# A linear attention stage rewritten: rotary sum in place in PSUM, state updates a unit ahead, head sums in four quarters, an own order for each engine

## What is computed

```python
q, k, v = x @ Wq.T, x @ Wk.T, x @ Wv.T            # 16, 4 and 4 heads of 128
q = q * cos + rotate_half(q) * sin                # k likewise
qf, kf = elu(q) + 1, elu(k) + 1
# scan over the tokens, causal, per head:
state = state + kf[:, None] * v[None, :]
z = z + kf
out = (qf @ state) / (qf @ z + EPS)
x = layernorm(x + out @ Wo.T)
x = layernorm(x + ffn(x))      # Hadamard, up and gate, silu, Hadamard, down
```

## Time and profile before

| | us |
|---|---|
| median of 3 runs (2710.3 to 2711.7) | 2710.74 |
| the profiled execution | 2705.35 |
| its span, first to last instruction | 2703.6 |

### The profile page before, as it was taken

The page is one execution under the profiler, slowest core; times in us unless marked ns, Lnnn a source line. Parts: engine busy times, 40 slices in busy tenths (PEclk is TensorE's granted clock), DMA queues, the critical chain, the costliest instruction groups (busy, mean ns, idle before and its releaser), DMA issues. The chain is left out here.

```text
span 2703.6 us, 32657 instructions
## 1 busy us (share of the span) xinstructions
PE 2523.3 (93%) x10689; PEld 1933.0 (71%) x10689; DVE 1671.2 (62%) x2283; ACT 1042.8 (39%) x1820; POOL 782.5 (29%) x661
## 2 busy tenths in 40 slices
PE   4899999999999999959999968999999999999997
PEld 3566666666666666638888857888888888888886
DVE  7587878787878787866767744443434343444444
ACT  2455555555555555532333323322222222222221
POOL 4365656565656565631112100000000000000000
PEclk8899999999999999979999989999999999999999
DMA  6111010101010101046676623210101000000000
GB/s 218 41 36 51 35 51 32 54 31 55 31 55 31 55 31 51 32 166 260 235 262 236 241 87 121 101 48 0 47 9 38 16 31 16 31 16 31 16 31 16
DMA packets 85163, 198.79 MB, mean 74 GB/s; under 512 B 8320, under 2 KB 25728, under 8 KB 74112
## 3 DMA queue, kind: packets, MB, share of 16 engines
q1 hardware_dynamic: 85120, 198.24, 20.6%
HBM read 134.77 MB, written 63.44 MB: 73 GB/s over the span
## 5 line engine op out<-in xcount | busy, mean ns | idle before, releaser
L1193 DVE SCALAR_TENSOR_TENSOR th<-th,pgu 128x512 f32<-128x512 f32 x128 | 88.1, 688 | 414.7 <-ACT th L1136 414.6
L1241 POOL TENSOR_TENSOR rstdc<-vec,neghalfc 128x1 f32<-128x1 f32 x32 | 17.5, 548 | 1063.9 <-DVE vec L1181 1063.9
L1136 ACT ACTIVATE th<-pgu,sg 128x512 f32<-128x512 f32 x128 | 88.1, 688 | 480.7 <-PE pgu L1074 480.7
L605 POOL TENSOR_TENSOR tb<-tb,sinb 128x512 f32<-128x512 f32 x160 | 219.3, 1375 | 131.5 <-ACT tb L489 130.6
L772 PE MATMUL py<-woh,oh 128*128 128x512 f32 x512 | 203.3, 397 | 27.8 <-DVE ol L891 27.8
L1074 PE MATMUL pgu<-x2h,wgh 128*128 128x512 f32 x512 | 201.0, 393 | 15.6 <-DVE x2l L1223 15.6
L609 POOL TENSOR_TENSOR Ql<-tb,Qh 128x512 fp32r<-128x512 f32 x128 | 180.8, 1418 | 116.0 <-ACT Qh L498 116.0
L422 PE MATMUL pj<-xh,wqh 128*128 128x512 f32 x512 | 207.9, 406 | 3.8 <-DVE ta L536 3.8
L493 ACT ACTIVATE tb<-ta 128x512 f32<-128x512 f32 x160 | 100.9, 630 | 268.6 <-DVE ta L540 268.3
L1074 PE MATMUL pgu<-x2h,wgl 128*128 128x512 f32 x512 | 202.6, 396 | 0.0
L1074 PE MATMUL pgu<-x2l,wgh 128*128 128x512 f32 x512 | 202.3, 395 | 0.0
(11 more groups left out here) (187 smaller groups left out, 6005.9 us busy)
## 6 DMA issues: line engine op xcount, KB each, us to landing
num_scratch<-no SPq DMA_DIRECT2D x128, 256.0 KB, 2.4
nt<-num_scratch SPq DMA_DIRECT2D x32, 1024.0 KB, 5.3
rb<-rden_scratch SPq DMA_DIRECT2D x32, 1024.0 KB, 5.9
x2st<-x_scratch SPq DMA_DIRECT2D x36, 256.0 KB, 3.7
xst<-in_xT SPq DMA_DIRECT2D x35, 256.0 KB, 3.8
xr<-in_x SPq DMA_DIRECT2D x32, 256.0 KB, 5.5
x_scratch<-x SPq DMA_DIRECT2D x32, 256.0 KB, 5.7
x_scratch<-x SPq DMA_DIRECT2D x8, 1024.0 KB, 4.3
```

What stands on the lines that cost most here:

```text
L605: nc.gpsimd.tensor_tensor(tb[s][:, :], tb[s][:, :], sinb[:, :], ALU.mult).then_inc(sin_done, 1)
L1136: nc.scalar.activation(th[s][:, :], pgu[2 * s][:, :], ACT.Tanh, scale=sg[:, f:f + 1]).then_inc(tanh_done, 1)
L1193: nc.vector.scalar_tensor_tensor(out=th[s][:, :], in0=th[s][:, :], scalar=1.0, in1=pgu[2 * s][:, :], op0=ALU.add, op1=ALU.mult).then_inc(g ...
L1241: nc.gpsimd.tensor_tensor(rstd[:, :], ve[:, :], neghalf[:, :], ALU.pow).then_inc(rc_done, 1)
```

## The change

- **Tables.** Each engine has a table of its own, so that each has its own order; SyncE gets one for its transfers. Waits name the number of things done so far in all tiles (`upto`), and every semaphore starts at one tile's worth.
- **Rotation.** The cosine product (`M`, now L525) is written back into the bank. `R` (L529) adds `tb` and 1.0 in place in the bank, by a scalar_tensor_tensor. `X` (L474) is Exp of the bank with bias -1 into `tb`; there is no Relu. `E` (L537) is the minimum of `tb` and 1, then the maximum with the bank, which gives the same function. The bank is free only after `E`. `I` is the sine product, `Q` the running sum, `P` the products with it, all as before but words of their own. `ta` is gone, `tb` has five buffers in place of three.
- **Banks.** `J`, `V`, `T` and now `D` share three banks `pj` in turn (`pden` is gone).
- **Sums.** `D` is one job for each group: four matmuls with a weight of ones of 32 columns, one for each head's product, each into its own 32 partitions of one bank (L425). `pr` has four buffers in place of two, and `Y` copies 128 partitions in place of 4.
- **State.** The state update is a kind of its own, `Z` (L439), and may stand ahead of the numerator of the unit before; `Sh` and `Sl` have two buffers each. `Kth` and `Ktl` have one in place of two.
- **Numerator out.** `O` is on ScalarE (L508) in place of VectorE.
- **Input.** The next tile's input is `H` in place of `X`; block 3 loads as soon as the low part of block 0 is made, since both use one buffer.

The core of the diff (waits and renamed semaphores left out):

```diff
 ORDER_PE = """
-C00 J11 C01 J12 U00 C02 C03 D04 J13 U01 J14 D11 U02 J20 D12 J21 U03 D13 T1 C10 J22 C11 C12 J23 U10 D14
+J21 C11 J22 J23 Z11 U10 J24 C12 D1 Z12 U11 J30 C13 Z13 U12 T2 J31 C20 J32 C21 J33 J34 U13 Z20 U20 Z21 C22 C23 D2
...
+NT = G + 1
 XS = 3
...
+NB = 3
+JOBS = [e for e in EVENTS["PE"] if e[0] in "JVTD"]
...
+                    elif kind == "D":
+                        pe.wait_ge(product, upto(m, d, H, g * G + G - 1))
+                        for i in range(G):
+                            q = slice(i * (P // G), (i + 1) * (P // G))
+                            last = nc.tensor.matmul(bank[q, :], onesd[:, :], pr[i][:, :], start=True, stop=True)
+                        last.then_inc(d_done, 1)
...
+                    elif kind == "Z":
+                        pe.wait_ge(t_lo, upto(m, d, KV, g))
+                        pe.wait_ge(v_lo, upto(m, d, NCH, c))
+                        pe.wait_ge(s_lo, upto(m, d, NU, u))
+                        for k, (a, b) in enumerate(((Kth, Vh), (Kth, Vl), (Ktl, Vh))):
+                            last = nc.tensor.matmul(pst[:, hd], a[:, c, :], b[:, c, hd], start=False, stop=(k == 2),
+                                                    skip_group_check=True)
+                        last.then_inc(state_done, 1)
...
-                    elif kind == "D":
...
-                        nc.tensor.matmul(pden[0:G, :], onesd[:, c - 1, :], pr[(c - 1) % 2][:, :], start=(c == 1),
-                                         stop=(c == G)).then_inc(d_done, 1)
...
-                        nc.scalar.activation(tb[s][:, :], ta[s][:, :], ACT.Exp)
-                        nc.scalar.activation(ta[s][:, :], ta[s][:, :], ACT.Relu).then_inc(relu_done, 1)
...
+                    elif kind == "X":
+                        act.wait_ge(rot_done, upto(m, d, NR, r))
+                        nc.scalar.activation(tb[c][:, :], pj[job_bank("J", g, c)][:, :], ACT.Exp,
+                                             bias=minus1[:, 0:1]).then_inc(exp_done, 1)
...
+                    elif kind == "O":
+                        act.wait_ge(unit_done, upto(m, d, NU, u))
+                        act.wait_ge(num_out[u % 2], m * (8 * NU) + (d + 1) * 8 * NU + 16 * (u // 2))
+                        nc.scalar.activation(no[u % 2][:].rearrange("p h t -> p (h t)"), pnum[u % 2][:, :],
+                                             ACT.Copy).then_inc(num_free, 1)
...
-                        nc.vector.tensor_tensor(ta[s][:, :], bank[:, :], cosb[:, :], ALU.mult).then_inc(bank_free, 1)
...
+                        nc.vector.tensor_tensor(bank[:, :], bank[:, :], cosb[:, :], ALU.mult).then_inc(cos_done, 1)
...
-                        nc.vector.tensor_tensor(ta[s][:, :], ta[s][:, :], tb[s][:, :], ALU.add).then_inc(rot_done, 1)
...
+                        nc.vector.scalar_tensor_tensor(out=bank[:, :], in0=bank[:, :], scalar=1.0, in1=tb[c][:, :],
+                                                       op0=ALU.add, op1=ALU.add).then_inc(rot_done, 1)
...
+                        nc.vector.scalar_tensor_tensor(out=(tb[c] if c else Kf)[:, :], in0=tb[c][:, :], scalar=1.0,
+                                                       in1=bank[:, :], op0=ALU.min, op1=ALU.max).then_inc(f_done, 1)
```

More of the change, by code:

```diff
@@ new lines @@
+Z22 U21 J00' U22 C30 C31 Z23 T3 U23 J01' Z30 C32 U30 J02' Z31 J03' J04' C33 U31 U32 V0' Z32 D3 J10' Z33 T0' C00'
+U33 C01' J11' Z00' C02' J12' V1' C03' J13' J14' U00' Z01' V2' V3' U01' Z02' J20' Z03' U02' T1' U03' C10' D0'
+Z10'
+"""
+ORDER_ACT = """
+N11 L20 S21 A11 S22 X21 S23 L21 N12 O10 X22 X23 S24 A12 L22 L23 N13 O11 X24 S30 L24 A13 N20 O12 K2 X30 S31 A20
+S32 X31 S33 X32 H0' S34 N21 A21 L30 H1' L31 N22 H2' O13 H3' X33 L32 A22 X34 L33 O20 A23 L34 N23 O21 S00' O22 A30
+N30 K3 A31 X00' O23 L00' S01' N31 A32 O30 X01' S02' N32 L01' S03' X02' S04' X03' L02' A33 L03' O31 X04' O32 L04'
@@ L97, in events_in, with jobs_before @@
     return [(w[0], int(w[1]), int((w[2:].rstrip("'")) or 0), int(w[-1] == "'")) for w in order.split()]
-EVENTS = events_in(ORDER_PE) + events_in(ORDER_REST)
+EVENTS = {"PE": events_in(ORDER_PE), "ACT": events_in(ORDER_ACT), "DVE": events_in(ORDER_DVE),
+          "POOL": events_in(ORDER_POOL), "SP": events_in(ORDER_SP)}
 NU = KV * NCH
[L102 to L106, removed]
-XS = 3
[L108 to L123, removed]
-def job_bank(kind, a, b=0):
[L127 to L144, removed]
+NR = KV * (G + 1)
+NT = G + 1
+XS = 3
+NB = 3
+JOBS = [e for e in EVENTS["PE"] if e[0] in "JVTD"]
+def job_bank(kind, a, b=0):
+    return [e[:3] for e in JOBS].index((kind, a, b)) % NB
+def jobs_before(kind, a, b, d, where):
+    bank = job_bank(kind, a, b)
+    order = [e + (body,) for body in (-1, 0) for e in JOBS if job_bank(*e[:3]) == bank]
+    back = order[:order.index((kind, a, b, d, 0))][::-1]
+    found = []
+    for e in back:
+        if where == "start":
+            if e[4] == 0 and e[3] == 1:
+                return found + [e]
+        elif where == "end":
+            if e[4] == -1 or e[3] == 0:
+                return found + [e]
+        else:
+            found.append(e)
+            if e[4] == 0 or e[3] == 1:
+                return found
+    return found
 def phase_a(nc, xT, wq, wk, wv, cosT, sinT, consts, wd, sd, wsd, num_d, den_d, wd_d):
@@ L356, in _ @@
                 pe.wait_ge(zeroed, 2)
[L357 removed]
+                nc.tensor.matmul(pst[:, :], Sh[0][:, :], xh[:, 0, :], start=True, stop=True,
                                  skip_group_check=True).then_inc(state_zero, 1)
@@ L474, in _, with body @@
+            bodies(pe, "PE", body)
         @block.scalar
         def _(act):
-            def body(m, events):
-                for e in events:
-                    kind, g, c, d = e
+            def body(m, events, where):
+                for kind, g, c, d in events:
                     u = g * NCH + c
-                    if kind in BANK_READS:
-                        bank = pj[job_bank(BANK_READS[kind], g, c)]
-                        act.wait_ge(job_done, job_number(BANK_READS[kind], g, c, m, d) + 1)
+                    r = g * (G + 1) + c
@@ L595, in _, with body @@
+            bodies(dve, "DVE", body)
         @block.gpsimd
         def _(pool):
-            def body(m, events):
-                for e in events:
-                    kind, g, c, d = e
-                    s = (g * (G + 1) + c) % NT
-                    if kind == "S":
-                        if (g, c) == (0, 0):
+            def body(m, events, where):
+                for kind, g, c, d in events:
+                    u = g * NCH + c
+                    r = g * (G + 1) + c
+                    if kind == "I":
+                        if r == 0:
```

367 lines of the change are left out of this document (182 added, 185 removed).

## The result

| | median, us | ratio to before | 95% interval |
|---|---|---|---|
| before | 2710.5 | | |
| after | 2523.5 | 0.931 | 0.9294 to 0.9327 |

The change saves 187 us. The forecast was 2567 us, its range 2500 to 2650; the measured time lies in the range, and it is the value of rival A within a microsecond.

The account below looks back on a forecast made before the run. TensorE was taken as the bound, VectorE close behind. Sums (-7.8) and state order (-10.1) gave -17.9 us a tile, times 8 is 143: from 2705.4 to 2562, plus 5.4 to the median, 2567 us; range 2500 to 2650.

Parts of the forecast that it names:

- rival A: Denominator sums: the four quarters run side by side, 1.2 us a job, tile 113.7 us, 2523 us in all; chance 0.27.
- The sums: Denominator matmuls on TensorE: quarters overlap only partly, 2.6 us a job, four jobs 10.4 in place of 18.2, -7.8 a tile.
- the ends: Start and end of the changed stage, 283.2 us: two tiles and 8.8 us, which were kept unchanged.
- State updates a unit ahead: TensorE's order: 6.7 us of waits for `Sl` go, and all but 0.7 of the clock's 4.1: -10.1 us a tile.
- Rotation in PSUM, copies on ScalarE: Rotary sum and numerator copies: VectorE falls to 82.1 us, ScalarE to 73.9; off TensorE's path, worth 0, only cover.
- Three banks held longer: Shared banks held until `E`: 5.0 us without queues against gaps of 6.2 to 8.2, so no wait, 0 taken.
- the walk: Jobs J11 to J14 followed through three queues: `E` ends at 5.5 of 6.2 us, no wait, 0.7 us to spare.
- Input block 3: Next tile's block 3, loaded after the first low part: 7 us of work within 8.7 of other matmuls, covered by 1.7.
- B: Denominator sums: the quarters run one after the other, 4.0 us a job, tile 124.9 us, 2612 us in all; chance 0.12.
- C: TensorE's waits come back elsewhere, as bank or score waits with the clock: tile 129.4, 2648 us; chance 0.20 with E.
- E: Waits for `Sl` are VectorE's queue alone and only move to `Al` or `lo`; priced in C, chance 0.20 with C.
- D: Slower because the banks bind: at a hold of 11 us they cost 30 us a tile, 2807 us in all; chance 0.04.

## Why the prediction was right or wrong

**The sums: right in kind, mis-sized.** The term was -7.8 us a tile, with a job of 2.6 us. The step that failed is "the second pass blocks the next quarter's second", which came from "instructions start in order". The quarters run by themselves; the job costs 1.19 us in place of 2.6 and the term is -13.4, the bound that I gave for "fully side by side". This is 5.6 x 8 = 45 of the 43.5 us by which the forecast was too high; 0.3 x 8 = 2.4 and the 5.7 of the ends, both below, go the other way, and 6.9 come from the profiled executions, which lay 5.4 us below the median before and 1.5 above it after.

**State updates a unit ahead: the sum right, the cause only half.** The term was -10.1 us a tile for waits and clock. The tile fell by 137.2 - 114.0 = 23.2 us, of which the sums are 13.4; so 9.8 are left for everything else. But with the updates put back behind their numerators only 3.6 us of the kernel's time come back, 0.6 a tile. The step that failed is to book all of it on the order. The numerators' waits for `Sl` are 1.0 us a tile without the new order, none without the quick rotation, and 2.8 without both: each edit was nearly enough for these waits, and the order had little left to win once VectorE was quick. That the sum came out within 0.3 us a tile is luck.

**Rotation in PSUM, copies on ScalarE: right in duration, wrong in worth.** `R` and `E` at 0.69 us, VectorE at 82.1 and ScalarE at 73.9 were forecast; 0.70, 0.69, 84.8 and 75.0 were measured. "Worth 0 by itself" was the mistake: undone, they cost 42 and 65 us. I had written in the first part that the product of 1.55 us beside GpSimd is why `Sl` is late, and then booked the cure on the order of the state alone. An engine that is 74% (after) to 80% (before) busy is no cover when four queues wait for each other's heads.

**Three banks held longer: right within one us a tile.** The matmuls wait for `E` 8.5 us in the whole stage (L403 and L413 for `tb` and `Kf`), against the 0 that I took with 0.7 to spare in the walk. In the loop it is the one stop of 0.8 us at J00', behind the long low part of the input, which the walk of J11 to J14 did not pass. With a slow VectorE these waits rise to 4.5 us a tile, but freeing the banks early wins nothing.

**Input block 3:** its transfer is in time; VectorE takes the block up without a pause behind its last operation. The 1.2 us that a weight load waits for `xl` are the stop at J00' again: there the low part took 1.78 us.

**The ends: wrong by 5.7 us.** I kept 8.8; they are 14.5. Of this, 3.8 us are a numerator of the last tile that waits for its mask on GpSimd; the rest is not traced:

```profile
990.92 0.77 PE L450 MATMUL pnum<-Ah,Vh 128*128 128x512 f32 x1 [3.76 <-POOL Al L600]
```

**The rivals.** A came true for the sums, and its total, 2523, is the measured one. Its tile of 113.7 is close to 114.03; its other terms were the forecast's, so that it hit with 10 us a tile booked on one edit where two share them. B is refuted by the three runs with fewer quarters. C and E, that the waits are VectorE's queue, were right about the queue: but the change cures it, which I had taken as cover only, and "alone" is too much, since with a slow VectorE the new order still takes the numerators' waits for `Sl` away. D's mechanism, banks that bind, shows as soon as VectorE is slow, with 4.5 us a tile where D needed 18.

## What to carry to other kernels

Several small float32 matmuls with few weight columns are worth grouping into separate quarters of the array: the group costs as much as its fullest quarter. Where engines hand work round in a circle, a long operation or a copy that waits at the head of a queue costs time even on an engine that is 70% busy; keep one of VectorE's two inputs in PSUM where GpSimd works on SBUF, and ask of each queue what stands behind a wait. A wait that disappears does not say which edit removed it: undo the edits one at a time, and those that may stand in for each other also together.

## What the runs showed of the hardware that was not expected

- Eight passes of four float32 matmuls in four quarters take 1.06 us, their eight weight loads start 7 to 8 ns apart and are over within 0.16 us, and the order in which quarters are addressed does not matter (2543.9 and 2544.0 us).
- VectorE writes PSUM in place at 0.70 us for 128x512 float32, 0.01 more than with SBUF as the destination.
- Exp with a bias from a tensor takes 0.69 us with its input in PSUM, without bias and from SBUF 0.63. With the bias and its input in SBUF it takes 0.72 in the mean, so it is not the bank that costs.
- A bank freed earlier made the kernel 9 us slower.
- The kernel before with the copies on ScalarE has more waits of TensorE over six bodies than the kernel before (59.5 against 46.0 us), but shorter ones (1.5 against 2.6 us the longest for `Sl`), a granted clock of 1.00 against 0.98 there, and the same time.
